# Dequantising the feed-forward weights ahead of the first chunk's queries, with wide tables and two pairs of banks

## The chip, the cores and the metric

One core of a Trainium2 chip (trn2). The time is device microseconds (us) of one execution. The kernel before took 905.2 us (median of 3 runs, 905.16 to 906.35).

## The reference

A transformer block on x of 32 x 64 tokens by 512, with a context of the same shape:

```python
x = x + xattn(layernorm(x), ctx, ctx, Wq, bq, Wk, bk, Wv, bv, interference, amp, Wo, bo)
x = x + ffn(layernorm(x), qweight_gu, qzeros_gu, scales_gu, g_idx_gu, qweight_down, qzeros_down, scales_down, g_idx_down)

# xattn: q, k, v = y + 0.1*amp*einsum(y, interference), y = proj(x, W, b) as 16 heads x 8 x 4
#        softmax(q k / sqrt(8)) v for each head and each of the 4 states, then out @ Wo.T + bo
# ffn:   W = scales[g_idx] * (nibbles(qweight) - (nibbles(qzeros) + 1))[g_idx]   # 4-bit weights, 8 in a word
#        h = silu(x @ W_gate) * (x @ W_up);  h @ W_down       # 512 -> 2 x 1376 -> 512
```

There are 4 groups of scales and zeros for gate and up (2752 columns), and 10 for down (512 columns).

## The kernel before, in words

The tokens are worked on in 8 chunks of 256. Matrix products run in pairs of f16 halves (a high and a low one, three products each), so each weight and each activation is needed as two halves: ACT writes the high one, DVE or POOL the low one.

*Setup.* The interference matrix is folded into Wq, Wk and Wv by matmuls (`pe_setup` L397, `act_setup` L729, `dve_setup` L928), four matrices one after the other, with two sets of four PSUM banks in turn; Wo is only permuted (32 small copies on DVE, L985) and transposed. The absolute maxima of all weights, scales and biases and of the whole context (eight reductions, L998) give powers of two that scale everything: one all-reduce over partitions on POOL (L1297), then some 40 tiny DVE operations up to `scale_ready` (L1045). Behind them come the halves of the folded weights (ACT L749, DVE L1059).

*Chunk 0.* K, V and Q of the first 256 tokens (`pe_project` L475, `pe_rows` L487), then attention in four batches of 64 tokens: scores (L619), maxima on DVE (L1166), their transpose (L629), the scores again, turned and with the maxima subtracted (L638, L644), four exponentials on ACT (L849), their high halves on ACT (L856) and low halves on POOL (L1368), the product with V (L661), the division (L1125, L1130). At the end comes the output projection (L492).

*Chunks 1 to 7.* The same attention, with the feed-forward network of the chunk before cut into 22 slots between its steps.

*Dequantisation.* The gate, up and down weights come in 14 pieces, cut into 35 units (24 of gate and up, 512 or 352 columns wide; 11 of down, 512 wide). A unit n is: DVE extracts a nibble from each word (`dve_dequant_int` L1072), ACT converts it to bf16 (L794), TensorE gathers the scale of each row's group in bank UB (L443, a one-hot matmul) and minus (zero + 1) plus the nibble in bank GB (L444, L446), ACT moves GB to SBUF with a scale (L777), DVE multiplies by UB (L1094), ACT writes the high half (L767) and POOL the low one (L1334). TensorE may start unit n once DVE has multiplied unit n - 1. In chunk 0 the slots that have no feed-forward work yet hold these units: a "tick" issues one step of each of several neighbouring units on each engine, and `ticks(slot)` spreads 38 ticks over slots 2 to 21.

*Order.* Each engine runs its instructions in the order in which the functions of that engine write them; only semaphores bind the engines together. The order of SP, which issues all DMAs, is written out in `sync_setup` (L346) and `sync_chunk` (L315). SP loads piece i once the nibbles of piece i - 2 are extracted (two staging buffers).

## Time and profile before

| what | value |
|---|---|
| median of 3 runs | 905.2 us |
| profiled execution: its own time, span | 906.32 us, 904.6 us |
| TensorE busy, share of the span | 772.6 us, 85% |
| DVE, ACT, POOL busy | 510.2, 438.3, 326.8 us |
| granted clock of TensorE, mean | 0.902 |
| first scores of chunk 0 (L619) start | 108.80 us |
| output projection of chunk 0 (L492) starts | 240.29 us |

The profile comes from one execution. Its clock is in parts of full speed: 0.5 is 1.2 GHz and 1.0 is 2.4 GHz. A row of a timeline gives start, duration, engine, line, operation, tiles, shapes and count; in brackets stands how long the engine was idle before it and what ended that. A duration of a row with a count spans all of its instructions. A row by stretch gives the stretch, its length, the busy time and count of PE, PE's weight loads, DVE, ACT and POOL, the granted clock, the busy share of the DMA engines and GB/s.

### The profile page before, as it was taken

The numbers are of one execution on the slowest core, as the hardware profiler recorded it, in microseconds if no ns is written. First come the engines' busy times: TensorE is split into PE (matmuls) and PEld (weight loads), VectorE is DVE, ScalarE is ACT, GpSimd is POOL, SyncE is SP. The second block draws the span as 40 slices with busy tenths as digits, with TensorE's granted clock in tenths as the row PEclk, the third lists the DMA queues.
The fourth block names the chain that finished last, engine by engine and source line by source line (L and its number), as shares of the span: only waits on it lengthen the run. The fifth ranks groups of instructions, "written<-read, shape, count | busy, mean of one in ns | idle before, by whom it ended". The sixth has DMA issues, their size and how long they took to land.

```text
span 904.6 us, 23874 instructions
## 1 busy us (share of the span) xinstructions
PE 772.6 (85%) x9953; PEld 562.3 (62%) x9953; DVE 510.2 (56%) x1013; ACT 438.3 (48%) x806; POOL 326.8 (36%) x290
## 2 busy tenths in 40 slices
PE   5306457766799999999999999999999999999898
PEld 5303323322278857876787778677857885787484
DVE  6987745554465646655574556456645663644421
ACT  1426355676365526662555455454635462655120
POOL 6732324555314530543064114412431352144220
PEclk9758655565599999999999999999999999999999
DMA  8900113222101011002100110011001100010000
GB/s 248 292 23 1 50 32 89 69 56 63 32 25 28 3 49 50 3 3 71 28 2 14 60 28 3 13 60 28 2 21 52 28 2 25 3 27 3 24 1 23
DMA packets 20702, 36.98 MB, mean 41 GB/s; under 512 B 3374, under 2 KB 7602, under 8 KB 20592
## 3 DMA queue, kind: packets, MB, share of 16 engines
q1 hardware_dynamic: 20604, 35.48, 13.5%
q8 instruction: 85, 1.39, 0.6%
q14 instruction: 13, 0.11, 0.0%
HBM read 26.56 MB, written 4.19 MB: 34 GB/s over the span
## 4 chain that ended last, share of the span: by engine, by line
PE 67%; DVE 15%; ACT 8%; issue 6%; DMA 2%; SPq 1%; DVEq 0%; ACTq 0%; POOL 0%
PE bank L511 16%; PE bank L526 13%; PE bank L482 9%; PE bank L492 9%; PE bank L644 4%; DVE nmf L1166 4%; PE bank L638 3%; PE bank L661 3%; ACT arena L849 3%; PE bank L619 2%; PE bank L459 2%; DVE arena L1094 2%; DMA arena<-in_L_xattn_Wo 2%; DVE arena L985 2%; PE bank L443 2%
## 5 line engine op out<-in xcount | busy, mean ns | idle before, releaser
L511 PE MATMUL bank<-arena,WGU 128*128 128x256 f16 (+1 forms) x2112 | 247.0, 274 | 1.4 <-DVE arena L709 1.4
L511 PEld LDWEIGHTS bank<-arena,WGU 128*128 128x128 f16 (+1 forms) x2112 | 206.2, 100 | 27.5 <-DVE arena L709 1.6
L1368 POOL TENSOR_TENSOR arena<-arena 128x512 f16<-128x512 f32 x128 | 147.0, 1173 | 190.5 <-ACT arena L856 190.5
L482 PE MATMUL bank<-arena,WT 128*128 128x256 f16 x768 | 91.3, 281 | 40.4 <-DVE arena L709 39.1
L526 PE MATMUL bank<-WD,arena 128*128 128x512 f16 (+1 forms) x528 | 121.1, 379 | 0.0
L849 ACT ACTIVATE arena<-bank,small 128x512 f32<-128x512 f32 x128 | 89.1, 776 | 58.3 <-PE bank L644 58.3
L1355 POOL TENSOR_TENSOR arena<-arena 128x512 f16<-128x512 f32 (+1 forms) x48 | 51.7, 1077 | 172.2 <-ACT arena L829 172.2
L482 PEld LDWEIGHTS bank<-arena,WT 128*128 128x128 f16 x768 | 76.9, 101 | 54.6 <-issue 43.1
L492 PE MATMUL bank<-WT,arena 128*128 128x512 f16 x384 | 88.0, 387 | 1.8 <-DVE arena L707 1.8
L526 PEld LDWEIGHTS bank<-WD,arena 128*128 128x128 f16 (+1 forms) x528 | 49.4, 98 | 53.2
L1166 DVE TENSOR_REDUCE nmf<-bank 128x8 f32<-128x512 f32 x128 | 79.4, 682 | 4.4 <-PE bank L619 4.2
L809 ACT ACTIVATE arena<-bank,bqk,small 128x256 f32<-128x256 f32 x64 | 38.4, 601 | 82.2 <-PE bank L482 82.2
L856 ACT ACTIVATE arena<-arena 128x512 f16<-128x512 f32 x128 | 71.9, 628 | 0.0
L813 ACT ACTIVATE arena<-bank,small 128x256 f16<-128x256 f32 x128 | 67.9, 608 | 0.0
L492 PEld LDWEIGHTS bank<-WT,arena 128*128 128x128 f16 x384 | 38.0, 99 | 47.4 <-issue 4.2
L1118 DVE SCALAR_TENSOR_TENSOR arena<-arena,small 128x512 f16<-128x512 f32 x64 | 45.2, 748 | 37.5 <-ACT arena L813 37.5
L644 PE MATMUL bank<-nmT,sel 32*128 32x128 f32 x1024 | 61.6, 317 | 0.0
L1125 DVE RECIPROCAL rinv<-bank 128x16 f32<-128x16 f32 x64 | 16.3, 255 | 78.1 <-PE bank L661 78.1
L1341 POOL TENSOR_TENSOR rstd<-vareps,small 128x1 f32<-128x1 f32 x32 | 19.6, 622 | 100.2 <-DVE vareps L1104 93.1
L1146 DVE SCALAR_TENSOR_TENSOR arena<-arena,small,bank 128x512 f32<-128x512 f32 (+1 forms) x48 | 33.6, 699 | 38.3 <-PE bank L511 37.1
L1142 DVE SCALAR_TENSOR_TENSOR arena<-arena,bank 128x512 f32<-128x512 f32 (+1 forms) x48 | 30.7, 639 | 41.9 <-ACT arena L825 41.9
L661 PEld LDWEIGHTS bank<-arena 128*128 128x128 f16 x1536 | 46.9, 97 | 9.7 <-issue 1.8
(157 smaller groups left out, 1068.8 us busy)
## 6 DMA issues: line engine op xcount, KB each, us to landing
arena<-in_L_ffn_qweight_gu SPq DMA_DIRECT2D x8, 688.0 KB, 5.4
arena<-arena SPq DMA_DIRECT2D x32, 144.0 KB, 3.0
WT<-in_ctx SPq DMA_DIRECT2D x8, 512.0 KB, 15.1
arena<-in_ctx SPq DMA_DIRECT2D x8, 512.0 KB, 3.7
arena<-in_x SPq DMA_DIRECT2D x8, 512.0 KB, 3.6
out_y<-arena SPq DMA_DIRECT2D x16, 256.0 KB, 2.1
arena<-in_L_ffn_qweight_down SPq DMA_DIRECT2D x10, 256.0 KB, 3.4
arena<-in_L_xattn_Wk SPq DMA_DIRECT2D x1, 1024.0 KB, 6.6
```

Of the source, the lines that this page charges most:

```text
L482: mm = e.matmul(jb[:, g2 * TOK:(g2 + 1) * TOK], WT[:, w, sp, kb, g * P:(g + 1) * P], src[:, mp, kb, :], start=(n == 0), stop=(n == 11))
L492: mm = e.matmul(jb[:, :], src[:, sp, kb, t * P:(t + 1) * P], WT[:, w, mp, kb, :], start=(n == 0), stop=(n == 11))
L511: mm = e.matmul(pb[0:m, i * TOK:(i + 1) * TOK], WGU[:, sp, kb, half * INTER + fb * P:half * INTER + fb * P + m], x2T[:, mp, kb, :], start= ...
L526: mm = e.matmul(pb[:, :], hT[0:m, sp, fb, t * P:(t + 1) * P], WD[0:m, mp, fb, :], start=(n == 0), stop=(n == 3 * FB - 1))
L644: mm = e.matmul(AB[a][:, i * P:(i + 1) * P], sel[rows, i, :], nmT[rows, :], start=False, stop=True)
L661: mm = e.matmul(JB[0][:, at:at + 2 * VCOLS], phl[:, a, part, i * P:(i + 1) * P], vv[:, b, :, 4 * i + a, v0:v0 + VCOLS], start=(n == 0), st ...
L813: ins = e.activation((qm, km)[w][:, 0, NB * g:NB * g + NB, v, :], src.rearrange("p (n t) -> p n t", n=NB), ACT.Identity, bias=BMASK[:, w, ...
L849: e.activation(pring[:, a, :], AB[a][:, :], ACT.Exp, bias=LIFT, scale=KSM).then_inc(S["exp_done"], 1)
L856: e.activation(phl[:, a, 0, :], pring[:, a, :], ACT.Copy).then_inc(S["p_hi"], 1)
L1166: e.tensor_reduce(nmf[:, a, 0:8], AB[a][:, :].rearrange("p (n k) -> p n k", n=8), AX_X, ALU.max, negate=True).then_inc(S["max_done"], 1)
L1355: e.tensor_tensor(flat(1), hbuf[0:m, u % 2, 0:cols], flat(0), ALU.subtract).then_inc(S["h_lo"], 1)
L1368: e.tensor_tensor(phl[:, a, 1, :], pring[:, a, :], phl[:, a, 0, :], ALU.subtract).then_inc(S["p_lo"], 1)
```

## The change

The dequantisation starts in the setup. The 40 ticks are placed by name: 22 in the setup, 4 behind K's projection, 12 behind V's, 2 in the first batch. Besides:

- The tables of gate and up are made from a wide layout (scales as 128 partitions x 86, zeros as 32 x 43 words) on DVE (`dve_tables`), and 16 DMAs inside SBUF bring them to the rows on which the one-hot matmul reads them. The one-hot of gate and up moves from POOL to DVE; the one of down stays on POOL, in four parts between the folds.
- The scale of the dequantised weights gets an all-reduce of its own at the start.
- Units alternate between two pairs of banks, so TensorE may start unit n once unit n - 2 is multiplied; the folds have four banks left and use them one after the other.
- The conversion to bf16 moves from ACT to POOL. Wo's permutation moves from DVE to ACT.
- SP loads the pieces between the weights and the context, each once the nibbles of the piece two before are extracted.

```diff
+TICKS = ND + 5
+PLACES = ["tables", "bias", "fold0", "fold1", "fold2", "fold3", "ctx2", "ctx4", "ctx6", "ctx8", "scales", "w0", "w1",
+          "keys", "values"] + list(range(SLICES))
+TICKS_AT = {"tables": 2, "bias": 2, "fold0": 2, "fold1": 2, "fold2": 2, "fold3": 2, "ctx2": 1, "ctx4": 1, "ctx6": 1,
+            "ctx8": 1, "scales": 2, "w0": 2, "w1": 2, "keys": 4, "values": 12}
+BATCH_TICKS = [IN_BATCH[0][2], IN_BATCH[0][3]]
+TWO_PAIRS = sum(TICKS_AT[p] for p in PLACES[:PLACES.index("values") + 1]) - 3
@@ sync_chunk, first chunk
+                load_next_piece(e, 8)
                 load_ctx(e, 1)
...
             v_dmas(e, c, first)
             if first:
-                for i in range(2, len(PIECES)):
-                    e.wait_ge(S["d_int"], units_before(i - 1))
-                    load_piece(e, i)
+                for i in range(9, len(PIECES)):
+                    load_next_piece(e, i)
@@ sync_setup, behind the small constants
+            load_piece(e, 0)
+            load_w(e, 1)
+            e.dma_start(gidx_d[0:96, :].bitcast(I32), gi_d.partition_broadcast(96)).then_inc(S["gid_loaded"], 16)
+            load_piece(e, 1)
+            e.wait_ge(S["sc_zeroed"], 2)
+            e.wait_ge(S["wide_ready"], 1)
+            for i in range(PARTS):
+                for g in range(GROUPS_GU):
+                    e.dma_start(sc3_gu[32 * i + g:32 * i + g + 1, :], sc3w[32 * g:32 * g + 32, i, :]).then_inc(S["sc_table"], 16)
+            e.wait_ge(S["zwide_ready"], 1)
+            for g in range(GROUPS_GU):
+                e.dma_start(z_gu[g:g + 1, :], zw[8 * g:8 * g + 8, :]).then_inc(S["z_table"], 16)
+            load_w(e, 2), load_w(e, 0)
+            load_next_piece(e, 2)
+            load_w(e, 3)
+            load_ctx_max(e, 0), load_ctx_max(e, 1)
+            load_next_piece(e, 3)
...
+        def load_next_piece(e, i):
+            e.wait_ge(S["d_int"], units_before(i - 1))
+            load_piece(e, i)
@@ pe_setup and pe_dequant
+            pe_ticks(e, "tables")
             e.wait_ge(S["t_ready"], 2)
...
+            pe_ticks(e, "bias")
             for i, w in enumerate(WORDER):
-                banks = bank[4 * (i % 2):4 * (i % 2) + 4]
                 e.wait_ge(S[f"w_loaded{w}"], 16)
-                reached(e, S["fold_evicted"], i - 1)
+                if i:
+                    e.wait_ge(S["fold_evicted"], i)
...
                 mm.then_inc(S["fold_done"], 1)
+                pe_ticks(e, f"fold{i}")
+            for place in ("ctx2", "ctx4", "ctx6", "ctx8", "scales"):
+                pe_ticks(e, place)
...
+        def pe_ticks(e, place):
+            for n in ticks(place):
+                pe_dequant(e, n - 2)
+        def dq_banks(n):
+            return (JB[0], JB[1]) if n < TWO_PAIRS and n % 2 == 0 else (GB, UB)
-            reached(e, S["d_w"], n)
+            reached(e, S["d_w"], n - 1 if n < TWO_PAIRS else n)
@@ act_setup
             for i, w in enumerate(WORDER):
+                if w == 3:
+                    act_permute(e)
                 e.wait_ge(S["fold_done"], i + 1)
                 e.wait_ge(S["wmax_done"], i + 1)
...
+                act_ticks(e, f"fold{i}")
+            for place in ("ctx2", "ctx4", "ctx6", "ctx8"):
+                act_ticks(e, place)
+            act_scale_part(e, 2)
+            act_ticks(e, "scales")
             e.wait_ge(S["scale_ready"], 1)
             act_whi(e, 0)
             act_hi(e, -1, "cT0"), act_hi(e, -1, "cT1")
+            act_ticks(e, "w0")
             act_whi(e, 1)
+            act_ticks(e, "w1")
+        def act_permute(e):
+            e.wait_ge(S["w_loaded3"], 16)
...
+                            ins = e.activation(wop[g][:, at:at + 64].rearrange("p (i q d) -> p i q d", i=KB, q=2),
+                                               ap(wraw[3][:, g], 0, P, 64 * hh + 32 * a + j, [(128, KB), (2, 2), (4, 8)]), ACT.Copy)
+        def act_ticks(e, place):
+            for n in ticks(place):
+                act_dequant_scaled(e, n - 2)
+                act_dequant_hi(e, n - 4)
@@ DVE and POOL
+        def dve_ticks(e, place):
+            for n in ticks(place):
+                dve_dequant_int(e, n)
+                dve_dequant_w(e, n - 3)
+        def pool_ticks(e, place):
+            for n in ticks(place):
+                pool_dequant_conv(e, n)
+                pool_dequant_lo(e, n - 5)
@@ pool_setup
+            e.wait_ge(S["maxq_ready"], 1)
+            e.partition_all_reduce(MRQ, MXQ, P, ABSMAX).then_inc(S["maxq_all"], 1)
...
+            for i in range(4):
+                pool_hot_d(e, i)
+                pool_ticks(e, f"fold{i}")
```

On DVE the tables come before the operations that build the folding matrix; a tick stands behind each weight's maximum twice, behind each second context maximum once, behind `scale_ready` twice, and twice behind each of the first two weights' low halves. `dve_tables` (some 25 operations) waits for the wide scales and zeros, the down scales, the group indices and POOL's all-reduce.

## Rows read from the trace of the kernel before

**Rows 1.** Busy time by stretch, first chunk from scores to output projection.

```profile
109.00:240.00 131.00, 82.55 (x837) 38.59 (x829) 68.93 (x128) 80.84 (x149) 57.79 (x52) 0.57 0.22 59
```

**Rows 2.** Chain that ended last, at the first chunk's end (start, us, what).

```profile
226.28 0.61 PE bank L443
...
228.00 0.70 ACT arena L777
...
229.46 0.61 PE bank L443
```

**Rows 3.** Timeline of the setup: start, us, engine, line, operation.

```profile
9.05 3.57 PE L403 MATMUL bank<-small,arena 128*128 128x1 f32 x16 [9.05 <-DVE arena L972]
...
14.33 11.94 PE L420 MATMUL bank<-arena 128*128 128x128 f32 x96
...
22.74 2.07 ACT L737 ACTIVATE arena<-bank 128x512 f32<-128x512 f32 x4 [1.51 <-PE bank L420]
...
36.72 3.64 PE L423 MATMUL bank<-ident,arena 128*128 128x128 f32 x16 [10.44 <-DVE arena L985]
...
42.93 9.08 DVE L998 TENSOR_REDUCE small<-WT 128x1 f32<-128x1024 f32 x8
...
52.05 0.16 DVE L1000 TENSOR_REDUCE maxima<-small 128x1 f32<-128x8 f32 x1
...
59.95 2.00 ACT L749 ACTIVATE WT<-arena,small 128x2048 f16<-128x2048 f32 x1 [17.49 <-DVE bv_row L1045]
```

**Rows 4.** Timeline, POOL's own operations.

```profile
13.15 1.33 POOL L1320 CAST WGU<-WGU 96x1376 f32<-96x1376 int32 x1 [6.38 <-DMA WGU<-in_L_ffn_g_idx_down]
...
27.72 3.82 POOL L1324 TENSOR_SCALAR arena<-WGU,small 96x1376 bf16<-96x1376 f32 x1
...
31.61 0.64 POOL L1320 CAST WGU<-WGU 96x512 f32<-96x512 int32 x1
...
60.00 1.12 POOL L1341 TENSOR_TENSOR rstd<-vareps,small 128x1 f32<-128x1 f32 x2 [7.14 <-issue]
...
120.17 1.16 POOL L1334 TENSOR_TENSOR WGU<-arena,WGU 128x512 f16<-128x512 f32 x1 [22.87 <-ACT WGU L767]
```

**Rows 5.** Single lines: ns min/median/max, first and last start.

```profile
L985 DVE COPY arena<-arena x32: 195/202/4866, 22.2 to 36.4; 128x64 f32<-128x64 f32 x32
...
L1083 DVE TENSOR_SCALAR arena<-arena,smalli x35: 394/486/1474, 112.7 to 233.4; 128x512 uint32<-128x512 uint32 x26, 128x352 uint32<-128x352 uint32 x8, 96x512 uint32<-96x512 uint32 x1
...
L1297 POOLq MODIFY_POOL_CONFIG  x2: 8/8/8, 40.0 to 40.0; - x2
```

**Rows 6.** Timeline, weights to first scores.

```profile
69.88 2.33 DVE L1059 SCALAR_TENSOR_TENSOR WT<-arena,small,WT 128x2048 f16<-128x2048 f32 x1
...
70.10 7.57 PE L482 MATMUL bank<-arena,WT 128*128 128x256 f16 x48 [26.49 <-DVE arena L709]
...
96.30 8.11 PE L482 MATMUL bank<-arena,WT 128*128 128x256 f16 x48 [12.57 <-DVE arena L709]
...
108.80 1.47 PE L619 MATMUL bank<-arena 32*128 32x128 f16 x48 [4.38 <-DVE arena L1118]
```

**Rows 7.** Timeline, one batch of the first chunk, its output projection.

```profile
110.29 2.49 DVE L1166 TENSOR_REDUCE nmf<-bank 128x8 f32<-128x512 f32 x4 [1.55 <-PE bank L619]
...
118.78 0.51 PE L638 MATMUL bank<-arena 32*128 32x128 f16 x12
...
122.41 2.78 ACT L849 ACTIVATE arena<-bank,small 128x512 f32<-128x512 f32 x4 [1.93 <-PE bank L644]
...
130.15 2.27 POOL L1368 TENSOR_TENSOR arena<-arena 128x512 f16<-128x512 f32 x2 [2.56 <-ACT arena L856]
...
240.29 7.79 PE L492 MATMUL bank<-WT,arena 128*128 128x512 f16 x24 [1.77 <-DVE arena L707]
```

**Rows 8.** SP's timeline, and DMA issues: KB each, us to landing.

```profile
97.79 3.18 SPq L312 DMA_DIRECT2D arena<-arena  x4
...
arena<-in_L_ffn_qweight_down SPq DMA_DIRECT2D x10, 256.0 KB, 3.4
```

More of the change, by code:

```diff
@@ L83, with ticks @@
 PARTS = 3
-TICKS = ND + 3
-FIRST_SLOT = 2
-TICK_ENDS = [0] * FIRST_SLOT + [TICKS * (k + 1) // (SLICES - FIRST_SLOT) for k in range(SLICES - FIRST_SLOT)]
-def ticks(slot):
-    return range(TICK_ENDS[slot - 1] if slot else 0, TICK_ENDS[slot])
+TICKS = ND + 5
[4 more added lines that the diff above has]
+BATCH_TICKS = [IN_BATCH[0][2], IN_BATCH[0][3]]
+assert sum(TICKS_AT.values()) + len(BATCH_TICKS) == TICKS
+TICKS_AT.update((k, 1) for k in BATCH_TICKS)
+TWO_PAIRS = sum(TICKS_AT[p] for p in PLACES[:PLACES.index("values") + 1]) - 3
+def ticks(place):
+    before = sum(TICKS_AT.get(p, 0) for p in PLACES[:PLACES.index(place)])
+    return range(before, before + TICKS_AT.get(place, 0))
 def width(block):
@@ L189, in build @@
         eye4 = take(16, F32)
+        early = [take(2048, F32) for _ in range(KB)]
+        bvx = take(2048, F32)
+        inter_all, inter_own, own = early[0][:, 0:HEADS * SUP * SUP], early[0][:, 256:512], early[1][:, 0:4 * SUP]
+        zraw_d = early[1][:, 4 * SUP:4 * SUP + DM // 8].bitcast(U32)
+        zint_d, scd = early[2].bitcast(U32), early[3]
+        rest_d = take(2048, F32)
         wop = [take(2048, F32) for _ in range(KB)]
-        bvx = take(2048, F32)
-        inter_all, inter_own, own = wop[0][:, 0:HEADS * SUP * SUP], wop[1][:, 0:HEADS * SUP * SUP], wop[2][:, 0:4 * SUP]
         take, pos = carver(max(pos[0], body0_end))
@@ L247, in build @@
         BMASK = small[:, 108:124].rearrange("p (w v k) -> p w v k", w=2, v=2)
+        MXQ, MRQ, BDQ, SCQ = (small[:, 124 + 2 * i:126 + 2 * i] for i in range(4))
         GM = small[:, 100:101]
@@ L539, in ffn_slice @@
                 if first:
[L540 to L541 removed]
+                    pe_ticks(e, k)
                     return
@@ L729, in act_setup @@
         def act_setup(e):
+            for i in range(2):
+                act_scale_part(e, i)
+            act_ticks(e, "tables")
             e.wait_ge(S["bias_done"], 1)
-            e.activation(bv_row[:, :], bank[5][:, :], ACT.Copy)
-            e.activation(bqk[:, :, :].rearrange("p a b -> p (a b)"), bank[4][:, 0:8], ACT.Copy).then_inc(S["bias_evicted"], 1)
+            e.activation(bv_row[:, :], bank[1][:, :], ACT.Copy)
+            e.activation(bqk[:, :, :].rearrange("p a b -> p (a b)"), bank[0][:, 0:8], ACT.Copy).then_inc(S["bias_evicted"], 1)
+            act_ticks(e, "bias")
             for i, w in enumerate(WORDER):
+                if w == 3:
+                    act_permute(e)
                 e.wait_ge(S["fold_done"], i + 1)
@@ L833, in act_slot @@
             if first:
-                for n in ticks(k):
-                    act_dequant(e, n)
+                act_ticks(e, k)
             else:
@@ L1327, in pool_dequant_lo, with pool_dequant_conv @@
+        def pool_dequant_conv(e, n):
+            if not 0 <= n < ND:
+                return
+            _, (blk, down, c0, cols) = DQ_UNITS[n]
+            m = width(blk) if down else P
+            e.wait_ge(S["d_int"], n + 1)
+            reached(e, S["d_gathered"], n - 1)
+            e.tensor_copy(wbf[n % 2][0:m, 0:cols], wint[n % 2][0:m, 0:cols]).then_inc(S["d_conv"], 1)
         def pool_dequant_lo(e, n):
@@ L1358, in pool_slot @@
             if first:
-                for n in ticks(k):
-                    pool_dequant_lo(e, n - 3)
+                pool_ticks(e, k)
             else:
@@ L1370, in pool_chunk @@
         def pool_chunk(e, c, first=False, last=False):
+            if first:
+                pool_ticks(e, "keys")
+                e.wait_ge(S["bo_loaded"], 16)
+                e.wait_ge(S["wlo_done"], 3)
+                pool_xres(e, 0)
+                pool_ticks(e, "values")
             pool_slot(e, c, 0, first)
```

267 lines of the change are left out of this document (152 added, 115 removed).

## The prediction, made blind

> **What bounds the kernel now.** I read the table of busy time by stretch first, then the chain that ended last, then the timeline of the first 110 us and of the first chunk, and last the single lines of the operations that the change moves. From chunk 1 on, TensorE is nearly always busy and the change leaves that part alone; the only time at stake lies ahead of the first output projection, at 240.3 us [rows 7]. It has two parts. The setup (weight folding, the maxima of all inputs, the scales, K, V and Q of chunk 0) lasts until the first scores at 108.8 us [rows 6]. The attention of chunk 0 follows, 131.5 us long, with the 35 units of dequantisation between its steps. There TensorE is busy 82.6 us of 131, the granted clock averages 0.57, and no engine is full [rows 1]: it is a chain. The reader sees its link in [rows 2]: a unit's first matmul starts at 226.28, ACT empties the bank at 228.00 (1.72 later), DVE multiplies for 0.70, and the next unit's first matmul starts at 229.46. So a unit costs 3.18 us, and 38 ticks at 3.18 make 121 of the 131.5. One pair of banks serialises PE, ACT and DVE.
>
> **The change part by part.** Two amounts are set against each other: what chunk 0's attention gives back, and how much later its first scores start.
>
> *What the attention gives back.* Only two ticks remain in it. A batch is then its own chain: scores 1.5, four maxima 2.5 [rows 6, 7], turning and copying the maxima about 0.9, the turned scores 3.6 (from 118.78 to the first exponential at 122.41), four exponentials 2.8. That is 11.4 from one batch's scores to the next. Transposes between these steps add about 0.5 in batches 0 and 3 and 3.2 in batch 2, where the second waits for the halves of the first. Four batches: 4 x 11.4 + 4.2 = 49.8. Behind them the last values wait for POOL's four low halves, two take 2.27 [rows 7]: 0.7 + 4.5, then values, division, a transpose and its two halves, 4.5: 9.7. Together 59.5, against 131.5: 72.0 less. The ends: 66 less (each batch 1.5 longer from the two ticks, chunk 1's layer norm and POOL) to 80 less (if the clock rose in it).
>
> *What stands ahead of the bias matmuls.* DVE builds the wide tables before the matrix that folds the weights: a wait for the scale table until about 6.3, some 25 small operations of 0.2 on the mean (5.1), a wait for POOL's early all-reduce and three more operations (to about 13.7), two extractions at 0.49 [rows 5]. The 4.8 us that led to the first matmul at 9.05 [rows 3] come after it: 19.5. Bias matmuls 5.3 (9.05 to 14.33 [rows 3]): 24.8. POOL's first conversion and the tables' 16 DMAs are there by then. Two units at 1.7 each: the first fold starts at 28.2 instead of 14.3. The ends: 24 and 32.
>
> *The four folds.* The fold of a matrix is 32 matmuls, a third of 11.94, so 4.0; its eviction 2.1 [rows 3]. Now one set of four banks serves all folds, and two ticks follow each: 7.2 at least on TensorE. POOL needs more. Its one-hot of the down groups, five operations from 13.15 to 31.54 = 18.4 [rows 4], is spread over the four stages, 4.6 each, ahead of that stage's two ticks. A POOL tick is now a conversion and a low half: 0.64 (the cast of 96x512, its nearest row) + 1.16 [rows 4] = 1.8. So 8.2 a stage. DVE can't work around it: a copy of 202 ns took up to 4866 beside such a POOL operation, and an extraction of 486 up to 1474 beside a low half [rows 5], so an extraction waits for POOL. Three stages and one unit on PE and ACT (2.9): 28.2 + 24.6 + 2.9 = 55.7. Then ACT does Wo's permutation, 32 copies of 128x64. On DVE one takes 202 ns [rows 5]; on ACT the bounds are 0.15 and 0.3, I take 0.2: 6.5. It stands behind stage 2's ticks in ACT's order, so nothing hides it, and the fold of Wo, PE's ticks, the eviction and DVE's multiplication of unit 8 queue behind it: 3.6 [rows 3] + 2.1 + 0.7 + 0.7 = 7.1. DVE reaches the context maxima at 69.3 (ends 60 and 75). The permutation's 14 us leave DVE, but there they stood beside loads.
>
> *Maxima and scales.* Eight maxima 9.1 [rows 3], three ticks on DVE at 0.49 + 0.69 = 1.2, and 0.5: the last maximum is out at 82.4, against 52.2 [rows 3]. From there to the scales took 7.7 (52.2 to 59.95); one more tick: 8.9, so 91.3.
>
> *Scales to K.* Before: 10.2 (59.95 to 70.10 [rows 6]). Now ACT's two ticks stand ahead of the first weight half, and the second needs DVE's tick behind the scales: 1.2 + 1.7 + 1.3, then ACT's half 2.0 [rows 3], DVE's 2.3 [rows 6], the context's halves 1.4: 9.9. The places "w0" and "w1" repeat it, as TensorE takes their ticks before K: 1.2 + 1.7 + 1.3 + 2.0 + 2.3 + 1.2 + 1.7 = 11.4. K starts at 112.6, 42.5 later than before.
>
> *K to the first scores.* Before 38.7 (70.10 to 108.80). Now K's first evictions and the third weight's halves, 12.1, a DVE tick 1.2, three units on PE 5.0: V starts 18.3 behind K. ACT then has 1.3 + 2.7 + 2.0, DVE 2.3 + 1.4 + 2.1, and with the waits V's halves are ready at 30.2. Here is a new wait: SP must issue the four stacking DMAs (3.2 for the same four [rows 8]) before it may issue the piece that the next unit reads: 0.9 to issue, 3.4 to land [rows 8]: 7.5, uncovered, as DVE's next instruction is that extraction and POOL, PE and ACT wait for it. From 37.7 nine units come at POOL and DVE's common rate. Their operations exclude each other, 0.28 to 0.49 + 0.64 + 1.16, so 2.2, in place of 3.18; with the last unit's trip 4.3: 22.0. X's halves 2.6; and from Q to the scores 12.5 as before (96.30 to 108.80 [rows 6]). Sum 74.8; the scores start at 187.4.
>
> *The sum.* 187.4 - 108.8 = 78.6 later; 78.6 - 72.0 = 6.6 longer. The profiled execution took 906.3 with a span of 904.6, 1.1 over the median of 905.2; against its own time the sum gives 912.9, and against the median 911.8. I say 912. The ends of one side (80 given back, maxima reached at 60, no wait for the piece) sum to -18, those of the other (66, 75, conversions at 1.6) to +30; they are not all reached together.
>
> The terms never seen here are the POOL conversion from uint32 to bf16 (0.64 to 1.6, as a one-input POOL operation with bf16 output on 96 rows takes 3.82 for 1376 columns [rows 4], 1.4 for 512) and the small table DMAs. At 1.6 a POOL tick is 2.8 and the scores start some 12 us later still; at 0.3 each stage gains 0.7.
>
> **A rule against the change.** POOL's only all-reduce is preceded by configuration instructions at 40.0 [rows 5], and POOL stands idle from there to 52.4, where DVE's maximum releases it; behind it POOL is idle 7.14 us with no releaser before its next operation at 60.00 [rows 4]. In the trace neither costs anything. The Trainium skill, GPSIMD Engine Reference, section 2.1 (Instruction dispatch), says that the first call to a freshly loaded kernel pays about 6 us for loading it. By that rule, the early all-reduce would come no sooner than about 12 us, and my 13.7 has room for it; were the library lost between the two, the second would be late by some 4 more, and the sum would be 916. The 12.4 us of idle time would cover such a load, so the trace neither bears the rule out nor speaks against it.
>
> **The rivals.** (A) The forecast: POOL's order and ACT's permutation pace the folds, 912.
> (B) POOL is worse than that: the 7.14 us behind an all-reduce comes between the second one and its tick, and conversions take 1.4 rather than 0.64, so POOL's tick costs 2.6. 5 from the first, 0.8 for each of nine units in "values" and a part of the others: 912 + 13 = 925. For it: conversion is an unseen form on POOL. Against it: the cast in [rows 4] is the same kind of work.
> (C) Faster: the folds are paced by TensorE alone. Its clock was full there (4.0 a fold against 3.6 for half as many transposes [rows 3]), so a unit is 1.0 and a stage 6.0; if POOL's one-hot runs beside the ticks and the permutation is through before TensorE needs it, the context maxima are reached at 28.2 + 24 + 3 = 55, 14 earlier: 898. It decides at the permutation: once DVE's first context maximum starts before 62.7, the change wins. For it: ACT was busy little in the setup. Against it: the order of ACT and POOL is written out, and the exclusion in [rows 5] is measured.
> (D) Both amounts cancel: the fold stretch and the piece's wait each come 3 shorter: 905. Also here: the table path is so late that units hardly move ahead, and nothing is given back that was not taken.
>
> **How the numbers follow.** About 0.2% (1.8 us) is what a measurement of this kernel can tell from no change. A 0.45 (906 to 920), B 0.18 (920 to 931), C 0.25 (893 to 903), D 0.12; of A and D some 0.02 each falls over the bounds. So faster 0.27, same 0.1, slower 0.63. The range 894 to 930 leaves out two tenths; the likeliest case alone is 906 to 920.
>
> **What would show it.** First fold near 28, first context maximum near 69, K near 113, scores near 187, output projection near 247, each on the timeline. DVE extractions of over 3 us in the folds (an extraction that waits for POOL's one-hot); 32 ACT copies directly ahead of Wo's transposes; a DVE gap of some 7 us ended by the DMA of a down piece; units about 2.2 us apart in "values"; batches of 11 to 15 us. I am wrong if units in the folds run without gaps on DVE, if the scores start before 181 (then it is faster), or if a batch still takes over 20.

## The result, and the profile after

The changed kernel took 913.64 us (median of 4 runs, 911.88 to 913.84) beside 905.47 for the kernel before (4 runs, 905.16 to 906.35) on the same chip: a ratio of 1.0084, 95% interval 1.0067 to 1.0102, so 0.8% slower. The forecast was 912.0 with a range of 894 to 930. The profiled execution took 913.65 with a span of 911.9.

The table of busy time by stretch, for the first chunk's attention (188 to 248) and for the same stretch as [rows 1]. Columns: the stretch and its length, then busy us and count of each engine, granted clock as a share, DMA share, GB/s.

```profile
188.00:248.00 60.00, 32.75 (x732) 27.03 (x732) 24.12 (x60) 24.70 (x45) 20.09 (x19) 0.59 0.03 11
...
109.00:240.00 131.00, 80.15 (x862) 45.77 (x862) 59.82 (x109) 63.14 (x110) 52.35 (x56) 0.62 0.13 39
```

The attention of chunk 0 now runs from 188.95 to 248.24, 59.3 us in place of 131.5. The second row is the stretch of [rows 1]: TensorE's total there hardly moves (80.15 us busy for 82.55), as the units still lie in it, now ahead of the attention; ScalarE's falls from 80.84 to 63.14.

The timeline of the changed kernel (start, us, engine, line, operation, the idle time ahead of it and what ended it), for the answers to [rows 3] and to [rows 6, 7]:

```profile
27.43 5.30 PE L466 MATMUL bank<-arena 128*128 128x128 f32 x32
...
37.53 2.06 ACT L807 ACTIVATE arena<-bank 128x512 f32<-128x512 f32 x4 [9.17 <-DVE maxima L1060]
...
39.96 5.84 PE L466 MATMUL bank<-arena 128*128 128x128 f32 x32
...
48.05 3.81 PE L466 MATMUL bank<-arena 128*128 128x128 f32 x32 [0.73 <-ACT arena L807]
...
59.33 6.55 ACT L829 ACTIVATE arena<-arena 128x64 f32<-128x64 f32 x32
66.02 3.65 PE L469 MATMUL bank<-ident,arena 128*128 128x128 f32 x16 [7.71 <-ACT arena L829]
...
72.68 2.34 DVE L1069 TENSOR_REDUCE small<-WT 128x1 f32<-128x1024 f32 x2
...
84.62 0.15 DVE L1074 TENSOR_REDUCE maxima<-small 128x1 f32<-128x8 f32 x1
...
95.89 0.49 DVE L1120 TENSOR_SCALAR bv_row<-bv_row,small 128x512 f32<-128x512 f32 x1
...
118.30 7.64 PE L546 MATMUL bank<-arena,WT 128*128 128x256 f16 x48
...
188.95 1.47 PE L683 MATMUL bank<-arena 32*128 32x128 f16 x48 [4.49 <-DVE arena L1229]
...
248.24 7.48 PE L556 MATMUL bank<-WT,arena 128*128 128x512 f16 x24 [1.54 <-DVE arena L771]
```

The reader sees the marks by which the change is measured: first fold at 27.43 (14.33 before), first context maximum at 72.68 (42.93), scales at 96.38 (59.95), K at 118.30 (70.10), first scores at 188.95 (108.80), output projection at 248.24 (240.29). The scores come 80.15 later, the attention is 72.2 shorter, and 7.95 is left; the medians differ by 8.17. What follows the output projection of chunk 0 is nearly the same in every kernel here: 663.6 to 665.2 us of the profiled span in all fourteen profiles (before 664.3, after 663.7). So the marks account for the profiled times.

GpSimd's timeline around its two all-reduces, and the line of the second one (min/median/max ns, first and last start):

```profile
20.54 1.14 POOL L1407 TENSOR_TENSOR arena<-arena 96x512 f32<-96x512 f32 x1 [8.85 <-issue]
...
89.76 0.43 POOL L1419 PARTITION_ALL_REDUCE maxima<-maxima  x1 [6.28 <-issue]
97.67 1.15 POOL L1465 TENSOR_TENSOR WGU<-arena,WGU 128x512 f16<-128x512 f32 x1 [6.93 <-issue]
...
L1419 POOLq MODIFY_POOL_CONFIG  x2: 10/10/10, 83.7 to 83.7; - x2
```

What [rows 4] showed as idle time behind the only all-reduce now stands on both sides of each: 6.28 of idle time ahead of the all-reduce (its configuration instructions stand at 83.7, 6.1 before it), and 6.93 more one cast later, both with "issue" as their end. The same pair stands around the early one (5.74, with its configuration at 5.6, and 8.85).

### The profile page after: what moved, and what is told of

Its sections match the earlier page's. It is cut to its first block, busy times and chain, and to the rows that moved or that the text cites. A ratio compares the mean times of both kernels' runs of the same rounds, so it can differ in the third digit from the quotient of the medians.

```text
span 911.9 us, 23901 instructions
## 1 busy us (share of the span) xinstructions
PE 777.4 (85%) x9953; PEld 565.0 (62%) x9953; DVE 490.1 (54%) x995; ACT 419.7 (46%) x800; POOL 322.8 (35%) x319
## 4 chain that ended last, share of the span: by engine, by line
PE 64%; DVE 12%; ACT 9%; issue 8%; POOL 3%; SPq 2%; DMA 1%; DVEq 0%; ACTq 0%; POOLq 0%
PE bank L575 16%; PE bank L590 13%; PE bank L546 9%; PE bank L556 9%; PE bank L708 4%; DVE nmf L1275 4%; PE bank L702 3%; PE bank L725 3%; ACT arena L925 3%; PE bank L523 2%; PE bank L683 2%; DVE stats L1210 1%; POOL arena L1456 1%; PE bank L693 1%; DVE arena L1194 1%
## 5 line engine op out<-in xcount | busy, mean ns | idle before, releaser
L725 PE MATMUL bank<-arena 128*128 128x34 f16 x1536 | 50.5, 180 | 10.1 <-POOL arena L1498 9.1
L725 PEld LDWEIGHTS bank<-arena 128*128 128x128 f16 x1536 | 46.6, 97 | 19.8 <-issue 7.9
```

The lines of the kernel that those rows point to most:

```text
L725: mm = e.matmul(JB[0][:, at:at + 2 * VCOLS], phl[:, a, part, i * P:(i + 1) * P], vv[:, b, :, 4 * i + a, v0:v0 + VCOLS], start=(n == 0), st ...
```

## The experiments

Each kernel is timed against the kernel before in the same session; the times compared with 913.6 are medians, and marks are read on the profiled timelines. The kernel before took 905.97, 905.44 and 905.70 in the three sessions of the experiments, beside the 905.47 of the result, so a gain over 913.6 is uncertain by about half a us from that alone. A profiled execution is one of the runs and can lie up to 2.7 us from its median; where that matters, the text says so. The cases are in the order in which they ran, except that e4b_second, of the last session, stands beside e4_allreduce.

### e1_piece: the pieces ahead of the stacking DMAs

```
             reached(e, S["pv_done"], SLOTS * c)
+            if first:
+                load_next_piece(e, 9)
+                load_next_piece(e, 10)
             v_dmas(e, c, first)
             if first:
-                for i in range(9, len(PIECES)):
+                for i in range(11, len(PIECES)):
                     load_next_piece(e, i)
```

> One edit to the changed kernel (913.65 in its profiled execution): in the first chunk SP issues pieces 9 and 10 ahead of the four stacking DMAs instead of behind them. Theory: the 7.19 us for which VectorE waits in 'values' for that piece lies on the path. With it gone the nine units there start 7.2 earlier, the stacking DMAs move 1.2 to 1.5 behind but the values are read only in the attention: first scores at 181.7 in place of 188.95, time 906.5 (905 to 908). Rival: TensorE and GpSimd only wait elsewhere later (Q's scores wait for the stacking, the clock falls with shorter gaps), then less than 2 comes back: 912 or more.

Measured: 906.72 (904.56 to 908.39), ratio 1.0007, 0.9997 to 1.0017. The two timelines, SyncE's queue and VectorE of the changed kernel first:

```profile
147.70 2.66 SPq L332 DMA_DIRECT2D arena<-arena  x4
...
154.87 0.49 DVE L1194 TENSOR_SCALAR arena<-arena,smalli 128x512 uint32<-128x512 uint32 x1 [7.19 <-DMA arena<-in_L_ffn_qweight_down]
```

```profile
155.03 0.75 DVE L1197 TENSOR_SCALAR arena<-arena,smalli 128x512 uint32<-128x512 uint32 x1 [1.27 <-DMA arena<-in_L_ffn_qweight_down]
```

In the changed kernel the extraction at 154.87 follows 7.19 us of idle time, in e1_piece the same moment finds four more extractions done and 1.27 us of idle time. First scores 182.51 in place of 188.95. The wait that the prediction had found in the order of SyncE's instructions was on the path, and its price was nearly right: this one order of issues is worth 6.9 us, beside a loss of 8.2. The result no longer differs from the kernel before (0.9997 to 1.0017).

### e3_permute: the permutation of Wo ahead of the first eviction

```
+PERM = {0: (0, 1, 2, 3)}
...
             for i, w in enumerate(WORDER):
-                if w == 3:
-                    act_permute(e)
+                act_permute(e, PERM.get(i, ()))
```

> One edit to the changed kernel: ScalarE's 32 copies that permute Wo stand ahead of the eviction of fold 0 (where ScalarE is idle for 9.17 us from 28.4 to 37.5) instead of ahead of the fold of Wo. Theory: TensorE's 7.71 us of idle time ahead of Wo's transposes at 66.0 goes, and Wo's fold starts as soon as GpSimd's and VectorE's ticks let it, near 60: the first context maximum at 67 in place of 72.68, the first scores at 183.5, time 908 (906.5 to 910). The copies want Wo, issued at 24.47 and there near 29, so 6.5 of them may reach 36 and cost the eviction nothing. Rival: GpSimd's last one-hot operation (60.17 to 64.1) holds VectorE's next extraction in any case, so what comes back is 2 or less: 911.5 or more.

Measured: 911.08 (909.22 to 912.20), ratio 1.0062, 1.0048 to 1.0075. First context maximum 69.85, 2.8 earlier.

```profile
35.74 6.57 ACT L831 ACTIVATE arena<-arena 128x64 f32<-128x64 f32 x32 [7.46 <-DMA arena<-in_L_xattn_Wo]
42.22 2.01 ACT L807 ACTIVATE arena<-bank 128x512 f32<-128x512 f32 x4
```

Wo is there only at 35.7, 10.8 us after its issue, so the copies end at 42.2 and the eviction of fold 0, at 37.53 in the changed kernel, comes 4.7 late. TensorE no longer waits ahead of Wo's transposes (7.71 us in the changed kernel), and 2.6 came back: that wait less the late eviction, 7.71 - 4.7 = 3.0. Neither theory's number: the copies were on the path, but the new place was not free.

### e4_allreduce and e4b_second: no all-reduce on GpSimd

The lines that begin with # name the engine; the new lines are cut to what each engine does.

```
-            e.partition_all_reduce(MR, MX, P, ABSMAX).then_inc(S["max_all"], 1)
+        # TensorE
+            e.transpose(bank[2][0:n, 0:P], src, ident[:, :]).then_inc(S["mx_turned"], 1)
+            e.wait_ge(S["mx_diag"], which)
+            e.matmul(bank[2][:, P:P + n], ones[0:n, :], mdiag[0:n, 0:n], start=True, stop=True).then_inc(...)
+        # VectorE
+            link(e, e.tensor_reduce(IV[0:n, 0:1], bank[2][0:n, 0:P], AX_X, ALU.max))
+            e.tensor_scalar(mdiag[0:n, 0:n], ident[0:n, 0:n], IV[0:n, 0:1], None, ALU.mult).then_inc(...)
+            e.wait_ge(S["mx_spread"], which)
+            link(e, e.tensor_copy(dst, bank[2][:, P:P + n]))
```

> The changed kernel with both of GpSimd's all-reduces replaced: TensorE turns the maxima (128 x 2, 128 x 11), VectorE takes the maximum of each row and multiplies it onto an identity, TensorE spreads that to all partitions with a matrix of ones. Theory: each all-reduce costs the kernel a configuration ahead of it (5.74 and 6.28 idle on GpSimd) and an idle stretch behind it (8.85 and 6.93). Without the second the scales are reached about 3 earlier (VectorE waited 2.44 for it) and the unit on which GpSimd sat until 97.67 is 3 or more earlier: K at 112 in place of 118.3. Without the first the first units start where VectorE's and TensorE's chains let them, 2 to 4 earlier. Together 905 (902 to 908), and no configuration instruction on GpSimd before 40 or at 83 to 98. Rival: the load is hidden behind other work, as my forecast had it for the second: then 1 to 2 us at most, 911.5 or more, since TensorE's and VectorE's extra steps cost some 1.5 each.

Measured: 910.90 (909.55 to 911.74), ratio 1.0056, 1.0042 to 1.0069. A gain of 2.7, between the two theories; K at 115.17 came 3.1 earlier and the first scores 3.6, though the first fold came later, at 27.99. To part the two all-reduces, the second alone:

> The changed kernel with only the second all-reduce replaced by TensorE and VectorE; the early one stays on GpSimd. With both replaced the time was 910.9. Theory: all of that gain is the second one's: the first unit waits for the small table DMAs until 24.5 whatever GpSimd does, and VectorE's steps of the first replacement only moved the bias matmuls 2 later. So K starts at 114.6 and the time is 910.4 (909 to 911.8). Rival: the idle stretch of 8.85 us behind the early all-reduce counted too: 912.5 or more.

Measured: 910.37 (908.18 to 911.06), ratio 1.0050, 1.0036 to 1.0064; K at 115.54. The second one alone gives 3.3 (3.5 against the kernel before of its own session, where both together gave 3.2), so the first one brought nothing that these runs can tell. GpSimd in e4b_second, and what ScalarE waited for in the changed kernel:

```profile
89.08 1.16 POOL L1483 TENSOR_TENSOR WGU<-arena,WGU 128x512 f16<-128x512 f32 x1
90.19 1.13 POOL L1490 TENSOR_TENSOR rstd<-vareps,small 128x1 f32<-128x1 f32 x2
```

```profile
98.91 0.55 ACT L870 ACTIVATE arena<-bank,small 128x352 f32<-128x352 f32 x1 [13.30 <-POOL WGU L1465]
...
102.49 1.99 ACT L841 ACTIVATE WT<-arena,small 128x2048 f16<-128x2048 f32 x1
```

Without the all-reduce GpSimd's low half at 89.08 and the powers at 90.19 run back to back; in the changed kernel the low half waited until 97.67, ScalarE (13.30 idle, ended by it) could not reuse its buffer before 98.91, and the first weight half stood behind that, at 102.49 (99.73 in e4b_second). The scales themselves came only 0.5 earlier (95.86 for 96.38), since VectorE's and TensorE's steps take about as long as VectorE's wait of 2.44 for the all-reduce; 2.2 of the 2.8 by which K is earlier lie behind the scales.

### e5_hot_dve: the down groups' one-hot on VectorE

```
-                pool_hot_d(e, i)            # GpSimd, folds 0 to 3
+            dve_hot_d(e)                    # VectorE, the same five operations, ahead of:
             dve_ticks(e, "bias")
```

> One edit to the changed kernel: the one-hot of the down groups, 18.4 us of GpSimd's time in five operations spread over the four folds, is computed by VectorE ahead of its ticks of 'bias', where VectorE is idle for 5.36 us. Theory: the folds are paced by GpSimd's order and by the extractions that wait beside its one-hot (2.55, 4.13, 3.32 in place of 0.48, and the 7.23 of the zeros). VectorE's five operations of 96x1376 cost 5 to 8 us, of which 5 lie in its gap; each fold stage then costs 6 to 7 in place of 8 to 10: first context maximum near 62 (58 to 66) in place of 72.68, time 903 (900 to 908). Rival: TensorE's fold matmuls and the permutation pace the folds, then the first context maximum comes at 69 or later and the time is 910 or more.

Measured: 904.08 (902.32 to 904.93), ratio 0.9979, 0.9970 to 0.9988: the largest single part, 9.6, and alone enough to turn the change's sign. First context maximum 62.08 in place of 72.68. The changed kernel's rows beside GpSimd's one-hot and the line of the extractions, then the same of e5_hot_dve:

```profile
27.57 7.23 DVE L1178 TENSOR_SCALAR arena<-arena 10x64 uint32<-10x64 uint32 x8
...
29.82 4.90 POOL L1440 TENSOR_SCALAR WD<-WD 96x1376 f32<-96x1376 f32 x1
...
L1194 DVE TENSOR_SCALAR arena<-arena,smalli x35: 395/480/4130, 12.2 to 167.9; 128x512 uint32<-128x512 uint32 x26, 128x352 uint32<-128x352 uint32 x8, 96x512 uint32<-96x512 uint32 x1
```

```profile
17.66 0.86 DVE L1179 CAST WD<-WD 96x1376 f32<-96x1376 int32 x1
...
27.62 1.35 DVE L1189 TENSOR_SCALAR arena<-arena 10x64 uint32<-10x64 uint32 x8
...
L1205 DVE TENSOR_SCALAR arena<-arena,smalli x35: 385/480/789, 12.3 to 157.1; 128x512 uint32<-128x512 uint32 x26, 128x352 uint32<-128x352 uint32 x8, 96x512 uint32<-96x512 uint32 x1
```

Two things went. VectorE does the five operations in 6.3 us of work from 17.66 on, where GpSimd took 18.1, and 5.36 of that stretch was idle time. And nothing of VectorE is held: the longest extraction is 789 ns in place of 4130, and the eight operations for the down groups' zeros, on 10 partitions of 64 numbers, take 1.35 in place of 7.23. How the 9.6 divides between the two was not separated; the zeros alone are worth 4.0 (e2_zeros).

### e3b_early: Wo on ScalarE's queue

```
@@ sync_setup
-            load_w(e, 3)
@@ act_setup
             act_scale_part(e, 0)
+            load_w(e, 3)
+            act_permute(e)
             act_scale_part(e, 1)
...
-                if w == 3:
-                    act_permute(e)
```

> The changed kernel with Wo loaded by ScalarE's own queue at about 8.9 us and permuted by ScalarE directly behind it, in the 12.93 us in which ScalarE waits for the scale table's rest (up to 21.72). When the copies stood ahead of the eviction of fold 0, ScalarE waited there for Wo until 35.7 and the eviction came 4.7 late; even so 2.8 came back. Theory: without that wait the whole of TensorE's idle time ahead of Wo's fold (7.7) goes: first context maximum at 65.5 (64 to 67) in place of 72.68, time 906.5 (905 to 908.5). Rival: the megabyte of Wo lands amid the 16 small table DMAs and Wk, the first unit (24.48) and the first fold (27.43) come 3 or more later, and the time is 910 or more.

Measured: 913.28 (911.73 to 914.68), ratio 1.0088, 1.0074 to 1.0102: no gain. First the DMA issues (KB each, median us to landing) of e3b_early, then two of its timeline rows:

```profile
arena<-in_L_xattn_Wo ACTq DMA_DIRECT2D x1, 1024.0 KB, 17.4
WD<-WGU SPq DMA_DIRECT2D x16, 5.4 KB, 12.8
```

```profile
28.23 0.59 PE L506 MATMUL bank<-WD,arena 68*128 68x512 bf16 x1 [5.10 <-DMA WD<-WGU]
...
35.28 4.59 PE L465 MATMUL bank<-arena 128*128 128x128 f32 x32
```

The rival was right, and its price was higher than it said: Wo took 17.4 us to land instead of 10.7, ScalarE stood until 25.60 with the second scale table queued behind the copies, and the first fold came at 35.28 instead of 27.43. The small tables landed late too (12.8 in place of 9.6; first unit 28.23 for 24.48). From 7 to 26 us the core's DMA engines moved about as much as in the changed kernel (280 and 203 GB/s from 7 to 17 and from 17 to 26, for 268 and 206): the second queue brought hardly more bytes, only another order. 7.9 was lost at the start and 9.1 regained by the first context maximum (71.45); of the 1.2 that this leaves, 0.6 is left at the output projection (247.66) and 0.4 in the median.

### e6_late: the placement undone

```
-TICKS_AT = {"tables": 2, "bias": 2, "fold0": 2, ..., "keys": 4, "values": 12}
+TICK_ENDS = [0] * FIRST_SLOT + [TICKS * (k + 1) // (SLICES - FIRST_SLOT) for k in range(SLICES - FIRST_SLOT)]
+TICKS_AT = {k: TICK_ENDS[k] - TICK_ENDS[k - 1] for k in range(1, SLICES)}
+TWO_PAIRS = 0
```

The pieces from 2 on are loaded behind the stacking DMAs again, as in the kernel before.

> The changed kernel with its placement undone: no unit of dequantisation in front of the first chunk's queries, all 40 ticks spread over chunk 0's 21 slots as before, on one pair of banks, pieces 2 on issued as before. The wide tables, the early all-reduce, the order of the loads and ScalarE's permutation stay. Theory: these cost little by themselves: Wo lands near 36, its permutation ends near 42, the context maxima end near 50, the second all-reduce adds 2 to 3 for its reload, K starts at 70 to 74 (70.10 before), the scores at 109 to 113, the attention takes 130 as before: 907 (905 to 910), so that the placement alone costs 4 to 9. Rival: what is put ahead of the bias matmuls (first fold at 23 instead of 14.3) and the late Wo carry the loss by themselves: K at 78 or later, 913 or more.

Measured: 926.08 (922.99 to 928.28), ratio 1.0225, 1.0205 to 1.0245: both theories wrong (the rival's "913 or more" came, but not by its mechanism, which had K at 78 or later). The setup was better than either said (K at 64.16, first scores at 98.33, 10.5 before the kernel before), and the attention worse: from 98.33 to 261.61, 163.3 us in place of 131.5. The largest wait of the attention, for e6_late and for the kernel before (engine, line, what it waited for, us in total, times, longest):

```profile
PE bank L497 <- DVE arena L1195: 75.8, 33, 5.9
```

```profile
PE bank L443 <- DVE arena L1094: 44.3, 25, 4.1
```

The change also spreads a unit over more ticks: TensorE takes unit n-2 (n-1 before), VectorE multiplies n-3 (n-1), GpSimd's low half is of n-5 (n-3). On one pair TensorE must wait for the multiplication of the unit before. In the kernel before VectorE did that multiplication one tick earlier; now it belongs to the same tick as TensorE's unit, so an attention step can lie between the two. That is a reading of the program; what the profiles show is 75.8 us waited in place of 44.3. These 31.5 are as large as the attention's 31.8, but a wait doesn't say what made it longer: the conversion on GpSimd (busy 75.6 us from 98 to 262, for 57.8 from 109 to 240 before) and the granted clock (0.53 for 0.57) differ too, and no run takes them apart. Against this kernel the early placement with two pairs costs 90.6 ahead of the scores (98.33 to 188.95), gives back 104.0 (163.3 to 59.3) and is worth 12.4 in the medians.

### e7_one_pair: one pair of banks, placement kept

```
-TWO_PAIRS = sum(TICKS_AT[p] for p in PLACES[:PLACES.index("values") + 1]) - 3
+TWO_PAIRS = 0
```

> The changed kernel with one pair of banks for every unit: the placement stays as changed. Theory: two pairs are worth most in 'values', where the units come 1.87 apart and one pair makes 3.18 of it (226.28 to 229.46 before): 12 ticks x 1.3 = 16, less the 7 us in which they wait for the piece: 9 to 16. In the folds the second unit of a stage waits for the first: 1 to 2 each in tables, bias, folds, scales, w0, w1, keys, some 10 more, of which half lies beside other work: 929 (922 to 938), first scores at 204. Rival: GpSimd's conversions and low halves pace the units in any case (1.8 each), then one pair costs 5 or less: 919 or less.

Measured: 945.84 (943.41 to 946.22), ratio 1.0448, 1.0433 to 1.0462. Two pairs are worth 32.2 us, twice what the theory said (its 929 means 15). On one pair the early placement is slower than the late one of e6_late by 19.8. Two multiplications in a row in "values", one pair and then two:

```profile
183.07 0.69 DVE L1205 TENSOR_TENSOR arena<-arena,bank 128x512 f32<-128x512 f32 x1 [1.80 <-ACT arena L870]
...
186.25 0.69 DVE L1205 TENSOR_TENSOR arena<-arena,bank 128x512 f32<-128x512 f32 x1 [1.79 <-ACT arena L870]
```

```profile
165.48 0.69 DVE L1205 TENSOR_TENSOR arena<-arena,bank 128x512 f32<-128x512 f32 x1 [0.53 <-ACT arena L870]
...
167.34 0.69 DVE L1205 TENSOR_TENSOR arena<-arena,bank 128x512 f32<-128x512 f32 x1 [0.53 <-ACT arena L870]
```

3.18 for 1.86, as [rows 2] had it. The first scores come at 217.74, 28.8 later. Ahead of K it costs 7.7, from K to V 4.9 (22.34 for 17.48), from V to Q 15.3 (56.85 for 41.55) and 0.9 behind it. The theory had "values" nearly right, but took 7 off for the piece, whose wait stays (7.45 here), and had the other places at less than half. The medians differ by 3.4 more than these 28.8, but little of that lies behind the first scores: the profiled execution (943.41) was 2.4 faster than its median, the attention took 58.9 (59.3 in the changed kernel), and what follows it 665.0 (663.7).

### e8_combo: four repairs together

The edits of e1_piece, e4b_second, e5_hot_dve and e3b_early.

> The changed kernel with four edits: pieces 9 and 10 issued ahead of the stacking DMAs (alone it took 6.9 us off 913.6), the down groups' one-hot on VectorE in 'bias' (alone 9.6), the second all-reduce replaced by TensorE and VectorE, and Wo loaded on ScalarE's queue at 9 us and permuted there. Theory: the four sit in different stretches (the piece in 'values', the one-hot in folds 0 to 2, the permutation at fold 3, the all-reduce at the scales), so they add: 913.6 - 6.9 - 9.6 - 2.7 - 7.5 = 887 (885 to 891), first context maximum at 54.5, scores at 160. Rival: with the one-hot and the permutation gone the folds meet TensorE's own pace and Wv's and Wq's landing, and the lighter GpSimd had already brought part of it: 893 or more.

Measured: 893.36 (891.65 to 895.25), ratio 0.9874, 0.9858 to 0.9890. The theory's 887 was missed by 6.4, and the measured time is the rival's "893 or more", though not for its reason. The first fold is again late, at 35.05, and the first context maximum, at 61.87, is where e5_hot_dve has it without the fourth edit (62.08): the fourth is worth nothing here either, as in e3b_early. 913.6 less 6.9, 9.6 and 3.3 is 893.8, so the other three add; no run holds these three alone.

### e2_zeros: the zeros ahead of the ticks

```
-            dve_ticks(e, "bias")
             dve_zeros_d(e)
+            dve_ticks(e, "bias")
```

> One edit to the changed kernel (913.6): VectorE's nine small operations for the down groups' zeros stand ahead of its ticks of 'bias', in its 5.36 us of idle time, instead of behind them, where eight of them took 7.23 us beside GpSimd's first one-hot operations (28.4 to 34.7). Theory: they cost 1.4 there, the maximum of Wk starts near 28 in place of 35.17, and the eviction of fold 0 near 33 in place of 37.5. The extraction behind the maximum still waits for GpSimd's operation (to 34.7), so a part is lost again: first context maximum at 69.5, time 910.5 (909 to 912). Rival: each fold stage is paced by GpSimd's own order, one-hot and ticks, and nothing comes back: 913 or more.

Measured: 909.61 (907.98 to 910.48), ratio 1.0045, 1.0031 to 1.0059; first context maximum 68.53.

```profile
17.66 0.92 DVE L1178 TENSOR_SCALAR arena<-arena 10x64 uint32<-10x64 uint32 x8
...
27.60 2.28 DVE L1060 TENSOR_REDUCE maxima<-arena 128x1 f32<-128x2048 f32 x1
29.80 5.18 DVE L1194 TENSOR_SCALAR arena<-arena,smalli 128x512 uint32<-128x512 uint32 x1
```

The theory's direction, with 4.0 for its 3. The last row shows what is left: the zeros are out of GpSimd's way, and now the extraction is held, 5.18 us for one of 0.48, until GpSimd's second one-hot operation is through (29.80 to 34.70). The reduction at 27.60 was over when that operation began; it ran beside GpSimd's cast of 1.33 us (28.37 to 29.70) and took its usual 2.28.

### e9_share and e10_actsplit: the permutation where ScalarE and GpSimd are idle

```
             load_w(e, 2), load_w(e, 0)
-            load_next_piece(e, 2)
             load_w(e, 3)
+            load_next_piece(e, 2)
...
+    # e9_share: ScalarE quarter i - 1 ahead of the evictions of folds 1 and 2,
+    #           GpSimd quarter 2 + i behind its ticks of folds 0 and 1
+    # e10_actsplit: ScalarE the quarters 0, 1 and 2 + 3 ahead of folds 1, 2, 3
```

The lines with # say in words what the other edits do. Both kernels hold the edits of e1_piece, e4b_second and e5_hot_dve.

> As the combination that took 893.4, but with Wo's permutation elsewhere: Wo is issued on the shared queue ahead of piece 2, ScalarE permutes one quarter ahead of the eviction of fold 1 and one ahead of that of fold 2, GpSimd the other two behind its ticks of folds 0 and 1. Theory: the combination lost 7.6 at its start, as Wo on ScalarE's queue landed at 25.4 only, ScalarE's scale table and TensorE's first fold waited for it (35.05 in place of 27.4), and the rest of its folds then ran as fast as TensorE allows (26.8 from the first fold to the first context maximum). With the first fold back at 27.4: first context maximum at 54.5 (54 to 58), time 886 (884 to 889). Rival: Wo lands after 40, or GpSimd's 16 small copies block VectorE and cost more than ScalarE's: 890 or more.

Measured: 885.28 (884.54 to 887.21), ratio 0.9781, 0.9766 to 0.9796, the fastest kernel of this study: 20.4 below the kernel before (905.70 in that session) and 28.4 below the changed one.

```profile
37.01 1.81 ACT L845 ACTIVATE arena<-arena 128x64 f32<-128x64 f32 x8
39.10 2.06 ACT L821 ACTIVATE arena<-bank 128x512 f32<-128x512 f32 x4 [0.28 <-PE bank L471]
...
37.24 2.16 POOL L1470 COPY arena<-arena 128x64 f32<-128x64 f32 x8
...
47.70 1.91 PE L474 MATMUL bank<-ident,arena 128*128 128x128 f32 x16
...
54.08 2.34 DVE L1087 TENSOR_REDUCE small<-WT 128x1 f32<-128x1024 f32 x2
```

The fold of Wo at 47.70 follows TensorE's tick without a gap (7.71 before it in the changed kernel), and the first context maximum is at 54.08, 8.0 earlier than in e5_hot_dve (62.08), which has the permutation in its old place.

> As e9_share, but with the permutation on ScalarE alone: a quarter ahead of the eviction of fold 1, a quarter ahead of that of fold 2, and the last half behind the ticks of fold 2 as in the changed kernel. Theory: the half left in front of Wo's fold costs its 3.3 us less what TensorE waits there in any case: first context maximum at 57, time 888.5 (886 to 891). If GpSimd's copies disturb VectorE, this one is the faster of the two.

Measured: 888.99 (888.26 to 891.68), ratio 0.9818, 0.9805 to 0.9831. Half of the copies on the path cost 3.7. The mark was at 60.04, not 57; this profiled execution (891.68) was 2.7 slower than its median, so the mark may be late by as much, and the time is the better witness. GpSimd's copies (270 and 246 ns each, ScalarE's 226) disturbed less than they saved.

## Why the prediction was right

It was right in time, in sign and in its mechanism: two amounts set against each other, one early, one late. None of its three signs of being wrong came, and the signs that it named did (extractions of over 3 us, the 32 copies ahead of Wo's transposes, a gap of 7 us ended by a down piece). That 912 lies within 2 us of 913.6 is luck in part, as errors of up to 4 cancel. By its own steps, forecast and measured:

- *What the attention gives back*: 72.0, measured 72.2 (131.5 to 59.3). The batches' scores start at 188.95, 200.71, 215.33 and 227.09, that is 11.8, 14.6 and 11.8 apart. (The five parts of a batch add to 11.3, not 11.4; it changes the sum by 0.4.)
- *Ahead of the bias matmuls*: first fold at 28.2, measured 27.43. Inside it, two errors cancel: the bias matmuls started at 17.68, not 19.5, but the tables' DMAs were not there by then, and the first unit waited for them until 24.48.
- *The four folds*: from first fold to first context maximum 41.1, measured 45.25 (mark at 72.68 for 69.3). The excess of 4.2 lies in the first stage: the folds start at 27.43, 39.96 and 48.05, so that stage took 12.5 for 8.2, and the second 8.1. From the third fold to the permutation it is 11.3 for 11.1, and from its end to the mark 6.8 for 7.1. The missing term is the down groups' zeros: counted at nothing, they took 7.23 beside GpSimd's first two one-hot operations, and e2_zeros gives 4.0 for them. The exclusion of VectorE by GpSimd was in the text for extractions (measured 2.55, 4.13 and 3.32) and not applied to the small operations between them. The permutation at 6.5 measured 6.55, TensorE's wait for it 7.71; no row on ScalarE stood behind the 0.2 us a copy, so that its 0.205 fits so well is luck too.
- *Maxima and scales*: last maximum out at 82.4, scales at 91.3; measured 84.77 and 96.38. From one to the other 11.6 in place of 8.9. The prediction had the second configuration lie in idle time, and gave 916 for the case that it didn't. GpSimd reached the configuration only at 83.7, where it had stood at 40.0 [rows 5], so the 6.28 lay partly open (VectorE waited 2.44), and behind it came 6.93 more, which rival B had. Together they are worth 3.3 (e4b_second).
- *Scales to K*: 21.3, measured 21.92, of which 2.2 are GpSimd's idle stretch behind the second all-reduce (19.68 in e4b_second). The rest was over-estimated by 1.6.
- *K to the first scores*: 74.8, measured 70.65. The wait for the piece was 7.5 and measured 7.19, on the path with 6.9 (e1_piece). The pitch in "values" was put at 2.2 and measured 1.86: that is 3 of the 4.2 too much. GpSimd's low half took 1.15, as forecast, and its conversion 0.61 alone and up to 0.81 there. In "values" its conversions follow each other 1.87 apart without idle time, so the extraction, which the text had added, costs almost nothing of its own.

So two errors of 4 with opposite signs, and a third of 3, all within the range. Rival B's mechanism was half there (its idle time behind the second all-reduce, but conversions at 0.61, not 1.4). Rival C was wrong as the changed kernel stands, but its threshold held: with the first context maximum at 62.08, before its 62.7, e5_hot_dve is faster than the kernel before (904.08 for 905.97). And e9_share comes to the mark that C named, 54.08 for 55, once one-hot and permutation are out of the way, though in a kernel with two more edits.

Of the rule in the Trainium skill, GPSIMD Engine Reference, section 2.1 (Instruction dispatch), by which the first call to a freshly loaded kernel pays about 6 us: the trace agrees for the call itself, with 5.7 and 6.1 us from the configuration to the all-reduce, and the second all-reduce paid it again. Behind the all-reduces these runs show 8.85 and 6.93 us more of idle time, the second of them after one cast.

## What to carry to other kernels

When work is moved ahead into a setup, list for each engine what already stands there and who holds it up or shares a queue with it: here 6.9 us hung on the order of DMA issues, 9.6 on five operations on the wrong engine, and some 8 on 32 small copies in front of a fold (an estimate: 62.08 to 54.08 at the first context maximum, or 8.6 from the sum of 893.8 to 885.3), and each could be moved into idle time that the trace shows. Try a new place together with its data's arrival: two of the three first places for the permutation waited for Wo. A deeper pipeline of units wants its second pair of buffers: on one pair it was slower, early (945.8) and late (926.1), than the kernel before (905). The old depth of a unit in the new places was not run.

## What the runs showed of the hardware

- An all-reduce on GpSimd costs some 6 us between its configuration and itself (5.7 and 6.1; in e6_late 5.6 twice) and 7 to 9 of idle time behind it (8.85 and 6.93; in e6_late 9.15 and 7.46). In the changed kernel one cast ran at 90.06, 0.3 behind the start of the second all-reduce, before the idle stretch began. With both replaced (e4_allreduce), neither stretch is there.
- Some VectorE operations are held until the GpSimd operation beside them is through, whatever their own size. Extractions of 0.48 us took 2.55, 4.13, 3.32 and (e2_zeros) 5.18, and each ended 0.2 to 0.3 us behind a GpSimd operation of 3.09, 4.86, 3.94 and 4.90. Of the eight operations on 10 x 64 numbers one took 4.90, the length of GpSimd's operation, and the eight together 7.23 for 0.92 alone. Not held: the multiplication by the bank (0.67 at 60.38, beside the operation of 3.94) and the 128 x 2048 reduction in float32 (2.27 to 2.28 in all four cases, one of them beside the first microsecond of the operation of 4.86).
- The five one-hot operations on 96 x 1376: GpSimd 1.33, 4.90, 3.09, 4.86, 3.94; VectorE 0.86, 0.87, 1.59, 1.71, 1.29.
- One megabyte on a second queue landed no sooner: 17.4 us from 8.14 on, while Wk, the tables and a piece were under way, and 10.7 from 24.5 on in the changed kernel, on SyncE's queue. The two stand at different places, so this is no comparison of the queues.
